# Second neighbour sum: slots moved out of the first three product tiles, bias rows copied by GpSimd

## The reference, cut to what matters

```
out = x @ root + bias
for r in range(8):
    mask = (edge_type == r)
    sums = segment_sum(x[src] * mask, dst)
    out = out + (sums / max(cnt, 1)) @ weight[r]
u = out
z = concatenate([u, x]) @ w_gate + b_gate
h = tanh(u) * z + x * (1 - z)
```

## Time and profile before

| what | us |
|---|---|
| median of 3 runs | 2672.86 |
| lowest, highest | 2669.37, 2674.23 |
| span of the profiled execution | 2721.5 |
| first product of the four units starts | 1810.6 |
| last product of them | 2243.7 |

### The profile page before, as it was taken

How to read it: one execution, slowest core, us unless ns; L and a number is a source line. 1 busy time by engine, 2 the same in 40 slices (tenths; PEclk the granted TensorE clock), 3 DMA queues, 4 the chain that set the end, 5 groups by cost and what they waited for, 6 DMA issues and landing times.

```text
span 2721.5 us, 29282 instructions
## 1 busy us (share of the span) xinstructions
PE 2462.5 (90%) x9679; PEld 1720.7 (63%) x9679; DVE 1640.9 (60%) x2605; ACT 867.5 (32%) x1550; POOL 806.2 (30%) x774
## 2 busy tenths in 40 slices
PE   5996888887999979999999999979999997967997
PEld 3552333554444438778888888868777775836786
DVE  8785666642124257655455546548888887856564
ACT  2001222331111124312212221228878774223232
POOL 1234666101111105655610000005444450003443
PEclk9997999998999989999999999989999998988999
DMA  4005666436334237533543453287787785447863
GB/s 146 1 24 174 177 183 180 109 142 221 103 96 136 88 134 263 186 133 112 193 158 135 146 197 135 100 296 231 245 264 236 262 262 186 130 176 282 314 245 143
DMA packets 195994, 472.58 MB, mean 174 GB/s; under 512 B 27960, under 2 KB 28760, under 8 KB 195880
## 3 DMA queue, kind: packets, MB, share of 16 engines
q1 hardware_dynamic: 105608, 230.09, 24.4%
q0 software_dynamic: 63008, 191.19, 22.5%
q10 hardware_dynamic: 27264, 49.88, 4.9%
HBM read 376.78 MB, written 100.43 MB: 175 GB/s over the span
## 4 chain that ended last, share of the span: by engine, by line
PE 72%; DVE 9%; DMA 9%; issue 5%; ACT 2%; another core or an unknown queue 1%; POOL 1%; DVEq 1%; SPq 0%; ACTq 0%; POOLq 0%
PE pair L1267 8%; PE pair L1269 8%; PE pair L1268 8%; PE pair L1147 6%; PE pair L1167 6%; PE pair L1054 4%; PE pair L993 3%; DMA tok_x<-x_rows,tok_list 2%; DMA rows_y<-y_rows,l_row 2%; PE pair L1285 2%; PE pair L1288 2%; PE pair L1015 2%; DVE U L1947 2%; PE pair L1033 2%; PE pair L1304 2%
## 5 line engine op out<-in xcount | busy, mean ns | idle before, releaser
L910 POOL DMA_INDIRECT rows_y<-y_rows,l_row x184 | 215.9, 1173 | 658.7 <-issue 453.6
L2274 DVE SCALAR_TENSOR_TENSOR low_y<-rows_y,l_inv,high_y 128x1024 fp32r<-128x1024 f32 x184 | 233.6, 1281 | 82.2 <-ACT high_y L1428 81.4
L1267 PE MATMUL pair<-sq_h,xh 128*128 128x512 f32 x700 | 273.9, 391 | 7.8 <-DVE sq_l L2188 7.8
L1269 PE MATMUL pair<-sq_l,xh 128*128 128x512 f32 x700 | 273.2, 390 | 0.0
L1268 PE MATMUL pair<-sq_h,xl 128*128 128x512 f32 x700 | 273.1, 390 | 0.0
L1428 ACT ACTIVATE sq_h<-quad 128x512 fp32r<-128x512 f32 x196 | 120.7, 632 | 465.5 <-PE pair L1269 437.7
L1428 ACT ACTIVATE high_y<-rows_y,l_inv 128x1024 fp32r<-128x1024 f32 x184 | 211.2, 1148 | 91.7 <-DMA rows_y<-y_rows,l_row 85.7
L893 POOL DMA_INDIRECT inv_ring<-inv_count,at_ring x184 | 189.3, 1029 | 74.6 <-issue 56.2
L856 POOL DMA_INDIRECT XT<-h_rows,l_src x184 | 177.0, 962 | 109.5 <-issue 44.4
L1054 PE MATMUL pair<-XT,XN 128*128 128x504 f32 x368 | 197.9, 672 | 0.0
L2188 DVE TENSOR_TENSOR sq_l<-quad,sq_h 128x512 fp32r<-128x512 f32 x196 | 129.7, 692 | 102.3 <-ACT sq_h L1428 74.6
(11 more groups left out here) (369 smaller groups left out, 5048.7 us busy)
## 6 DMA issues: line engine op xcount, KB each, us to landing
quad<-in_L_gnn_weight SPq DMA_DIRECT2D x28, 1024.0 KB
xh<-sum_parts SPq DMA_DIRECT2D x14, 1280.0 KB
xl<-sum_parts SPq DMA_DIRECT2D x14, 1280.0 KB
y_rows<-u ACTq DMA_DIRECT2D x70, 256.0 KB
tok_raw<-in_L_ffn_w SPq DMA_DIRECT2D x8, 2048.0 KB, 15.4
tok_raw<-in_L_ffn_w SPq DMA_DIRECT2D x16, 1024.0 KB, 16.1
exp_bg<-bias_gelu_rows SPq DMA_DIRECT2D x23, 512.0 KB
x_rows<-X SPq DMA_DIRECT2D x20, 512.0 KB, 6.4
```

The source lines that it names most:

```text
L910: pool.indirect_dma_start(rows_y[s % RING1][:], None, y_rows, bass.IndirectOffsetOnAxis(ap=l_row8[:, s:s + 1], axis=0)).then_inc(y_in[s % ...
L1267: mm(o, high[:, k, :], sq_h[:, k, :], start=(k == 0), stop=False)
L1269: last = mm(o, high[:, k, :], sq_l[:, k, :], start=False, stop=(k == KE - 1))
L2274: v.scalar_tensor_tensor(low_y[s % RING1][:], rows_y[s % RING1][:], l_inv[:, s:s + 1], high_y[s % 3][:].bitcast(F32), ALU.mult, ALU.subtra ...
```

## The change

Tiles 0 to 2 of unit 0 carry no slots. Tile 3 of it has four, tiles 4 to 9 have five. In units 1 to 3 tile 0 keeps two, tiles 3, 6 and 9 have four, and the other six have five. The last unit ends with six slots and not with eight. So the units have 38, 48, 48 and 50 slots, where they had 45, 45, 45 and 49. VectorE evicts tiles 0 and 1 before its first serve.

The bias row is loaded once into 128 partitions (bias_u), after M7's pieces in the last relation. GpSimd waits for M5 and copies it ten times into u_rows. bias_u lies where wl pieces 2 and 3 go, so VectorE waits for the copies before piece 2; ScalarE waits for them before its first slot.

```diff
-CHANGE, END = 4, 8
-def slot_steps(m):
-    return (5, 7) if m == 0 else (0, 2, 4, 5, 7) if m % 3 == 0 else (1, 3, 5, 7)
+CHANGE, END = 4, 6
+BARE = 3
+def slot_steps(j, m):
+    if j == 0 and m < BARE:
+        return ()
+    if m == 0:
+        return 5, 7
+    return (1, 3, 5, 7) if m % 3 == 0 and (j > 0 or m == BARE) else (0, 2, 4, 5, 7)
...
+        bias_u = place("bias_u", "w", [P, D], skip=10 * HALF)
...
@@ block.sync, relation loop
+                else:
+                    sp.wait_ge(wl_ready, pieces_at(r, M7) + 5)
+                    sp.dma_start(bias_u[:], a["L1_gnn_bias"].partition_broadcast(P)).then_inc(bias_u_in, 16)
                 sp.wait_ge(a_full, full_at(r, M7) + HT)
...
-            sp.wait_ge(x3_stored, 16 * NT)
-            sp.wait_ge(a_full, full_at(REL - 1, M5) + HT)
-            for m in range(NT):
-                sp.dma_start(u_rows[:, m, :], a["L1_gnn_bias"].partition_broadcast(P)).then_inc(u_init, 16)
...
@@ block.gpsimd, before the gathers
+            pool.wait_ge(bias_u_in, 16)
+            pool.wait_ge(x3_stored, 16 * NT)
+            pool.wait_ge(a_full, full_at(REL - 1, M5) + HT)
+            for m in range(NT):
+                pool.tensor_copy(u_rows[:, m, :], bias_u[:]).then_inc(u_init, 1)
...
@@ block.scalar
             act.wait_ge(inv_listed, 1)
+            act.wait_ge(u_init, NT)
...
@@ block.vector, last M3
                                     dve.wait_ge(wh_ready, 8 * SPLIT_ROOT + k + 1)
+                                    if k == 2:
+                                        dve.wait_ge(u_init, NT)
                                     v.tensor_tensor(wl[:, k, :], raw[:, k, :], wh[:, k, :].bitcast(F32), ALU.subtract).then_inc(wl_ready, 1)
...
-            dve.wait_ge(u_init, 16 * NT)
+            dve.wait_ge(u_init, NT)
+            for q in range(BARE - 1):
+                evict(q, 0)
             for s in range(AHEAD):
                 serve(s)
```

More of the change, by code:

```diff
@@ L51, with slots_before @@
 RING1 = 5
-CHANGE, END = 4, 8
-def slot_steps(m):
-    return (5, 7) if m == 0 else (0, 2, 4, 5, 7) if m % 3 == 0 else (1, 3, 5, 7)
-SLOT_AT = [sum(len(slot_steps(i)) for i in range(m)) for m in range(NT + 1)]
-UNIT_SLOTS = SLOT_AT[NT] + CHANGE
-assert SLOTS % RING == 0 and 4 * UNIT_SLOTS + END - CHANGE == SLOTS
+CHANGE, END = 4, 6
[6 more added lines that the diff above has]
+    return (1, 3, 5, 7) if m % 3 == 0 and (j > 0 or m == BARE) else (0, 2, 4, 5, 7)
+def slots_before(j, m):
+    return sum(len(slot_steps(i, n)) for i in range(4) for n in range(NT) if (i, n) < (j, m)) + CHANGE * j
+UNIT_END = [slots_before(j, NT) + CHANGE for j in range(3)]
+assert SLOTS % RING == 0 and slots_before(3, NT) + END == SLOTS
 REL = 8
@@ L432, in build @@
         (parts_in,) = sems(4, "parts_in")
-        u_init = sem("u_init")
+        u_init, bias_u_in = sem("u_init"), sem("bias_u_in")
         high_ready, low_ready, row_off_ready, hot01_ready = sem("high_ready"), sem("low_ready"), sem("row_off_ready"), sem("hot01_ready")
@@ L1308, in _ @@
                             last.then_inc(w_free, 1)
-                        if k in slot_steps(m):
-                            sum_slot(UNIT_SLOTS * j + SLOT_AT[m] + slot_steps(m).index(k))
+                        if k in slot_steps(j, m):
+                            sum_slot(slots_before(j, m) + slot_steps(j, m).index(k))
                 for s in range(CHANGE if j < 3 else END):
-                    sum_slot(UNIT_SLOTS * j + SLOT_AT[NT] + s)
+                    sum_slot(slots_before(j, NT) + s)
             pe.wait_ge(agg_ready, 2)
@@ L1662, in _ @@
                 nc.scalar.activation(hot01[:, s % RING, :], row_off[:], ACT.Relu, bias=ones[:, 0:1], scale=-1.0).then_inc(hot01_ready, 1)
-                j, at = divmod(s + 1, UNIT_SLOTS)
-                if at == 0 and j < 4:
+                if s + 1 in UNIT_END:
+                    j = UNIT_END.index(s + 1) + 1
                     for k in range(KD):
@@ L2320, in _ @@
                 for m in range(NT):
-                    for i in range(len(slot_steps(m))):
-                        s = UNIT_SLOTS * j + SLOT_AT[m] + i
+                    for i in range(len(slot_steps(j, m))):
+                        s = slots_before(j, m) + i
                         step(s, j * NT + m - (i < 1 and m > 0))
@@ L2326, in _ @@
                 for i in range(CHANGE if j < 3 else END):
-                    s = UNIT_SLOTS * j + SLOT_AT[NT] + i
+                    s = slots_before(j, NT) + i
                     step(s, (j + 1) * NT - (i < 1))
```

## The result

| | before | changed |
|---|---|---|
| median, us | 2671.11 | 2640.72 |
| lowest, highest (4 runs each) | 2662.76, 2674.23 | 2637.17, 2650.66 |
| ratio, 95% interval | | 0.990, 0.988 to 0.992 |
| span of the profiled execution | 2721.5 | 2634.9 |
| first product of the four units | 1810.6 | 1752.55 |

The change gains 30 us, 1.1%. The prediction said 5 us, and its range ended at 2659.

A forecast was written before the change was run, and what follows sets the result against it. TensorE, busy 90% of the span, was taken as the bound, so its idle time counted. The terms -18.0 + 1.8 + 11.4 - 0.5 = -5.3 us took 2672.9 to 2667.6 us, range 2659 to 2679.

The forecast's parts named there:

- Part 1: Three bare tiles at the start of unit 0: 19.0 us of loss becomes a 1.0 us wait, -18.0 us.
- Part 3: Denser tiles: 24 five-slot tiles lose 0.8 us each against 7.8 now, +11.4 us; fewer four-slot tiles, -0.5.
- Ring rival: Five-slot tiles in a row let the five rows_y buffers set the pace: 1.35 us a tile, 2680.8 us; chance 0.31.
- Loose rival: Five-slot tiles lose only 0.4 us each, -14.9 us in all, 2658.0 us; chance 0.18.
- Part 2: Moved slots: two more before the last product, +1.8 us; the same gate_raw transfer covers those behind it, changes of unit stay.
- Part 4: Bias rows by ten GpSimd copies of 1.24 us, hidden behind 13.9 us before wl piece 2: 0, up to +10.9 us.
- Late copies rival: GpSimd copies at 2.48 us each end late and hold up VectorE, +5.6 us, 2678.5 us; chance 0.06.

The follow-up runs named there:

- e1: The changed kernel's slots moved, but the ten bias transfers kept and no GpSimd copies; 2654.3 us, ratio 0.994 to the kernel before.
- e4: The changed kernel with bias_u loaded by ten transfers of a tenth of the columns each; 2705.3 us, ratio 0.993 to the kernel before.
- e9: Repeat of the kernel with only the slots moved and the ten bias transfers kept; 2705.3 us, ratio 0.995 to the kernel before.
- e11: Repeat of the changed kernel with bias_u loaded by ten small column transfers; 2696.8 us, ratio 0.992 to the kernel before.
- e12: The changed kernel with the four-slot tiles of units 1 to 3 put first, then six five-slot tiles in a row; 2698.7 us, ratio 0.992 to before.
- e14: The changed kernel once more, unaltered, on the chip of the five-slot row test; 2703.9 us, ratio 0.992 to the kernel before.
- e6: The changed kernel with eight slots at the end, two five-slot tiles of the last unit cut to four; 2702.4 us, ratio 0.993 to before.
- e15: Repeat of the changed kernel with eight slots at the end, two last-unit tiles cut to four; 2701.4 us, ratio 0.992 to before.
- e13: The kernel before, unchanged, profiled a third time; 2721.3 us, ratio 0.999.
- e2: The kernel before with only the GpSimd bias copies added, slots as before; 2658.4 us, ratio 0.996 to the kernel before.
- e5: The changed kernel's slots without GpSimd copies, one transfer filling the bias rows of all ten tiles; 2700.5 us, ratio 0.993 to before.
- e10: The changed kernel once more, unaltered, beside the bias transfer variants; 2703.3 us, ratio 0.994 to the kernel before.
- e0: The kernel before, unchanged, profiled once more; 2671.1 us, ratio 1.000.
- e3: The changed kernel once more, on the chip where its two halves were tried singly; 2649.4 us, ratio 0.991 to the kernel before.

## Why the prediction was wrong

**Part 1 held in its sum, and not in one step.** Predicted -18.0 us; the two stretches lost 19.06 before and 0.35 after, so -18.7. The predicted 1.0 us of waiting came to nothing, since low_y is ready 17.1 us after the first product and was ready after 20.6. The prediction looked for that gain in the last store, which should shrink from 7.57 us towards 4.1. Of the 3.5 us the store gives only 0.7 (the first gather is issued 10.2 us after the first product and was at 10.9); 2.6 come from the gather, which takes 4.4 us and not 7.05, and which the prediction had left as it was. So that the wait came out near its low end is in part luck: the traffic was the right cause, and the transfer that it slowed was another. In e1, with the old traffic, the wait was 1.96 us, within the predicted 0 to 3.0.

**Part 3, the five-slot tiles, is the step that failed.** Predicted was +11.4 us (24 tiles at 0.8, against 7.8 now). The windows of the 24 tiles, two pairs of unit 3 and the sum:

```profile
2079.95:2089.92 9.97, 9.97 (x45) 1.00 0.84 253
2089.92:2101.06 11.14, 10.68 (x45) 1.00 0.83 268
...
2140.01:2149.98 9.97, 9.97 (x45) 1.00 0.88 268
2149.99:2161.14 11.15, 10.72 (x45) 1.00 0.82 262
sum 249.80, PE 245.29; mean PE 10.22
```

They hold 1052 matmuls (the last tile of unit 0 up to its last product), 238.5 us, so 11.3 lost, 0.47 a tile: +3.5 us. Over four profiles of the changed kernel the mean is 11.0, over three of before 6.3, so +4.7. The pair shows the structure: the first tile takes 9.97, just its matmuls, the second 1.17 more. Over eight profiles of kernels with pairs (the changed kernel's four, e1, e4, e9, e11), 72 first tiles lost 0.13 us each and 72 second ones 0.82. Right in the prediction was that a five-slot tile leaves the ring of five no room, and its 0.8 is the price of a second tile. What it had wrong is to whom it applied it: it raised the price of all 24 tiles, with the words that a first tile behind a four-slot one "is the case measured". But the first tiles of pairs lose hardly anything, and ten of the 24 tiles are such (nine in units 1 to 3, and tile 4 of unit 0). The measured case was misread as well. The old five-slot tiles, each behind two four-slot ones, lost 0.43 to 0.65 on average, but a third to a half of it lies in one of them: tile 6 of unit 2 lost 2.6, 2.2 and 2.5 us in the three profiles of before, the other eleven 0.24 to 0.47 on average.

A reading that fits the pairs: four-slot tiles build up a lead of the gathers, the first tile of five uses it up, the second pays, and a wait once paid lets the gathers run ahead again. e12's unit 2, which paid in all six tiles, shows that this isn't the whole of it. Nor is it the gather that most waits of a second tile end with. The last wait of the last pair in the changed kernel, from the chain of waits and the timelines of ScalarE, VectorE and TensorE:

```profile
2146.57 6.24 DMA rows_y<-y_rows,l_row
...
2156.39 1.14 ACT L1442 ACTIVATE high_y<-rows_y,l_inv 128x1024 fp32r<-128x1024 f32 x1
...
2157.00 0.68 DVE L2315 TENSOR_TENSOR OS<-pair,XN 128x512 f32<-128x512 f32 x1
2157.60 1.21 DVE L2299 TENSOR_TENSOR X<-pair,X 128x1024 f32 x1
2158.73 2.47 DVE L2291 SCALAR_TENSOR_TENSOR low_y<-rows_y,l_inv,high_y 128x1024 fp32r<-128x1024 f32 x2
...
2160.15 0.70 PE L1299 MATMUL pair<-high_y,hot 128*128 128x512 f32 x2 [0.40 <-DVE low_y L2291]
```

The slot's high_y is ready at 2157.53, but VectorE first does an eviction (evict) and a pair's addition (add_pair), and starts low_y 1.2 us later; a gather of 6.24 us, two slots earlier, stands at the head of the chain. In the four profiles of the changed kernel TensorE waited 21.7 us before slots of the 36 second tiles (68 waits of 0.04 us or more), and 16.1 us of it (48 waits) ended with a low_y that VectorE, busy with add_pair, started 0.45 to 1.5 us after its high_y. So the fixed order of VectorE's loop has a part that the prediction didn't price. A kernel in which it makes low_y before it adds the pair wasn't run, so how the loss divides between ring and order is open.

The Ring rival is out in the kernel as changed: the mean is 0.47 a tile, far from 0.95, and the worst tile lost 1.24 us (1.70 in e14, 2.4 in one tile of e4). e12, with longer rows, comes nearer to it: up to 2.0 in a tile, and 0.60 a tile on average. The Loose rival had nearly the right rate (0.4 a tile) and a chance of 0.18. Its 2658.0 us still lies 17 us over the time.

**Part 2 had one half right.** Two slots more before the last product: +1.8 us. The wait before slot 181 grew from 7.27 to 11.84 us, near the 4 us forecast, but by luck: the slots ahead of it are done 8.3 us sooner (6.2 us after the last product in place of 14.5) and the transfer has landed 3.8 us sooner. What the prediction missed: "the same transfer" isn't the same. It took 12.4 us and not 16.2, and the tail shrank by 3.2 us in place of 0 (3.4 as a mean of four profiles against three). I had taken the duration of a transfer as given, though the gathers beside it, which the edit moves, are part of it. e6 and e15 show it from the other side: with END = 8 the stage gains and the tail gives it back.

**Part 4 held.** 1.07 us a copy (10.74 for ten), predicted 1.24, all hidden behind 13.9 us; the Late copies rival is out. (The page's mean of 1130 ns counts their overlaps twice.) By the Trainium skill (GPSIMD Engine Reference, section 3.1) the best case of such a loop is about 1.8 cycles per element, an estimate of 1.54 us; the measurement differs and decides: 1.07 us for 1024 elements is 1.26 cycles of 1.2 GHz, nearer to the 1.03 that the same section gives as the bound by the ports.

The prediction's sentence on VectorE and GpSimd blocking each other can be checked here, though not at the wl pieces, since the copies had ended. The first two of the ten copies and the one subtraction of sq_l that falls on both (sq_l = quad - sq_h, two inputs in SBUF) take longer than all others of their kind, as it says; minimum, median and maximum in the changed kernel:

```profile
L2203 DVE TENSOR_TENSOR sq_l<-quad,sq_h x196: 678/692/1455, 1081.3 to 1739.1; 128x512 fp32r<-128x512 f32 x196
L915 POOL COPY X<-bias_u x10: 1037/1049/1500, 1738.6 to 1748.2; 128x1024 f32<-128x1024 f32 x10
```

The maximum of sq_l starts at 1739.10 while the first copy runs (1.44 us from 1738.56), and ends 0.6 us into the second. In all eleven profiles with the copies the first two take 1.44 and 1.49 to 1.50 us, the other eight 1.03 to 1.05, and this one sq_l 1.45 to 1.46; away from the copies none takes over 0.75. It cost 0.9 us of the cover and nothing in time.

**What wasn't priced.** The first tiles of units 1 to 3, behind the changes, lost 6.1 us before and 3.7 after, -2.4 (-1.5 as a mean of the profiles). The changes themselves are equal (36.5 and 36.7). Four-slot tiles: -0.8, predicted -0.5. So the stage adds up: -18.7 + 1.8 + 3.5 - 0.8 - 2.4 + 0.2 = -16.4, measured -16.3.

**The last stage, outside of all steps.** It takes more than one course. The windows of e13 (before) and e14 (changed), on one chip: the stage, the tail, the last stage.

```profile
1809.38:2240.86 431.48, 395.87 (x1660) 0.95 0.80 257
2240.86:2267.85 26.99, 14.04 (x37) 0.68 0.83 304
2463.35:2722.30 258.95, 231.26 (x1072) 0.94 0.66 236
```

```profile
1808.34:2225.79 417.45, 397.09 (x1669) 0.97 0.80 261
2225.79:2249.93 24.14, 9.42 (x29) 0.72 0.77 285
2445.60:2704.40 258.80, 230.57 (x1072) 0.95 0.66 235
```

Here the last stages are alike, and stage and tail make -14.0 - 2.9 = -16.9 us, against -18.4 in the times. That is what the change does where it acts. As means of all profiles of the two kernels (four and three) it is -13.8 - 3.4 = -17.2 us, 0.6%. In the first comparison the last stage took a short course. Waits of TensorE in its last 245 us, the changed kernel first, then e14; below each how tok_raw, the experts' weights, landed:

```profile
PE pair L1397 <- DVE tok_w1l L2485: 4.8, 3, 2.7
...
DMA to landing us min/median/max: 5.2/12.5/17.8
```

```profile
PE pair L1397 <- DVE tok_w1l L2485: 15.1, 4, 7.2
...
DMA to landing us min/median/max: 14.8/16.9/17.6
```

In the long course TensorE waits 10 us more (12 counted from its first up product) for the low parts of the experts' weights, these for ScalarE's high parts, and these for a transfer that lands later. In the timeline of SyncE single issues stall there: in e14 one small transfer takes 7.29 us to be issued and the two behind it 6.65, where in the changed kernel no such transfer takes over 2.8 and no two over 3.6.

```profile
2541.34 7.29 SPq L796 DMA_DIRECT2D U<-in_L_ffn_b  x1
2548.98 6.65 SPq L779 DMA_DIRECT2D tok_raw<-in_L_ffn_w  x2
```

Over the 18 profiles the length goes by how many such waits of over 5 us there are. With none the stage took 243.0 to 246.3 us (the changed kernel's first, e2, e5, e6, e12), with one 248.9, 249.3 and 255.4 (e10, e11, before), with two 258.0 to 259.8 (the ten others). A slow issue alone isn't enough: in e12 single issues take up to 4.5 us.

The times fit this too. On the chip of e0 to e3 the changed kernel's six runs are 2635, 2638, 2644 and 2654, 2655, 2657, and before's 32 lie between 2660 and 2680. The upper three give -15 us, the lower three some -30. But before's runs spread over 20 us as well, so it may have more than one course of its own.

**What stays open** is why such a wait comes. Two of the four profiles of the changed kernel have none or one (245.2 and 248.9 us), two have both; of the three of before one has one, two have both (255.4, 258.9 and 259.4). e4 and e11 are the same kernel, and so are e6 and e15, and each pair differs by 9 to 17 us: neither the number of bias transfers nor END decides it. That the change makes the waits rarer is possible, and not shown: 10.2 of the 29.7 us of the first comparison hang on it. A test that holds the landing of tok_raw fixed wasn't run.

In short: -5.3 us were forecast, and stage and tail gave -19.5 in the first profiles. Of the 14.2 us between them 7.9 lie in the five-slot tiles, 3.2 in the tail, 2.4 in the first tiles of the units and 0.7 at the start. The tiles alone would have left the time at the edge of the stated range (2672.9 - 13.2 = 2659.7 us); stage and tail together put it at 2653, and the last stage did the rest: of the -30.4 us in the times 10.2 lie there.

## What to carry to other kernels

When a pattern that stalls is to be used more often, don't price it by its mean: list its loss instance by instance, with what stood before each one and which engine ended the wait. Here one tile held a third or more of the old loss, and the first tiles of the new pairs lost 0.13 us each. A transfer's duration is no constant of the kernel: where an edit moves the traffic that ran beside it, price it anew, above all where the end waits for it. And look at a stage that the edit doesn't touch in several profiles of both kernels before its part of a gain is claimed or denied.

## What was unexpected in the hardware

- A copy on GpSimd, SBUF to SBUF, [128 x 1024] in fp32, takes 1.07 us in a row of ten; tensor_tensor of the same size takes 2.48.
- A store of 256 KB took 7.9 to 9.3 us beside ten bias transfers (e1) and 2.0 without them (changed kernel); a gather of 128 rows 7.3 to 8.3 and 4.4 to 6.0, though the bias transfers had landed when it was issued: they had held up the two lower-left transfers, which ran beside it.
- Where a GpSimd copy and a VectorE subtraction of two SBUF inputs meet, both take longer (1.50 for 1.04 us, 1.46 for 0.69).
- The same stage with the same instructions takes 243 to 260 us, by how the weights' transfers land.
- Chips differ by 50 us in this kernel, in its first neighbour sum and relation stage, for both kernels alike.
